# Routed tiles turned by VectorE from four strips, listed in the order of their rows, with the final loads released group by group

## The reference

```python
topk_p, topk_i = jax.lax.top_k(softmax(flat @ router_w.T), 2)      # 2 of 8 experts for each of 4096 tokens
topk_w = topk_p / topk_p.sum(-1, keepdims=True)
combine = zeros((T, 8)).at[arange(T)[:, None], topk_i].add(topk_w)
for e in range(8):                                                 # w_fc[e]: 512 x 128, w_proj[e]: 128 x 512
    out = out + (square(relu(flat @ w_fc[e].T)) @ w_proj[e].T) * combine[:, e:e + 1]
out = out + square(relu(flat @ shared_fc.T)) @ shared_proj.T
result = layernorm(flat + out)
```

## Time and profile before

| What | Value |
|---|---|
| Time, median of 3 runs | 490.98 us (490.75 to 491.0) |
| Profiled execution, first to last instruction (span) | 498.7 us |
| PE, DVE, ACT, POOL busy in the span | 454, 357, 354, 315 us |
| Mean DMA rate | 97 GB/s |
| 332.5 to 423.9 us (mostly full tiles): PE, ACT, DVE busy | 91.4, 61.9, 33.8 us |
| 470.4 us to the end (finish): length, PE busy | 28.3, 18.1 us |

### The profile page before, as it was taken

The page is one execution under the profiler, slowest core; times in us unless marked ns, Lnnn a source line. Parts: engine busy times, 40 slices in busy tenths (PEclk is TensorE's granted clock), DMA queues, the critical chain, the costliest instruction groups (busy, mean ns, idle before and its releaser), DMA issues.

```text
span 498.7 us, 7644 instructions
## 1 busy us (share of the span) xinstructions
PE 453.9 (91%) x2184; PEld 293.6 (59%) x2184; DVE 356.7 (72%) x873; ACT 354.5 (71%) x557; POOL 315.1 (63%) x285
## 2 busy tenths in 40 slices
PE   8997999999999988798898898489999999999983
PEld 5332444444344333455576675389999999899721
DVE  5898999999999999998688964353333333455246
ACT  3989999999999999815455555327667667566537
POOL 4754789999999999845566666604555455555421
PEclk9998999999999999989799999979999999999997
DMA  8031246654343434001111111131222222222095
GB/s 274 8 122 43 86 146 213 216 196 151 130 153 131 151 133 148 3 1 33 39 45 43 45 43 47 46 94 51 72 65 81 71 60 58 60 57 67 11 324 182
DMA packets 41193, 48.56 MB, mean 97 GB/s; under 512 B 5616, under 2 KB 25266, under 8 KB 41152
## 3 DMA queue, kind: packets, MB, share of 16 engines
q1 hardware_dynamic: 35792, 39.07, 23.8%
q0 software_dynamic: 5216, 8.70, 5.6%
q10 hardware_dynamic: 144, 0.31, 0.2%
HBM read 19.17 MB, written 29.11 MB: 97 GB/s over the span
## 4 chain that ended last, share of the span: by engine, by line
PE 40%; POOL 22%; DVE 16%; issue 8%; ACT 7%; DMA 2%; another core or an unknown queue 2%; DVEq 0%; POOLq 0%; SPq 0%; ACTq 0%
POOL memory_feat L495 17%; PE routed_ph L1500 13%; PE routed_po L1513 12%; PE dispatch_sph L998 4%; PE dispatch_spo L1008 3%; POOL memory_feat L503 2%; DVE memory_prod L769 2%; DVE memory_y_raw L778 2%; POOL memory_prod L518 2%; PE memory_nsum L620 1%; ACT finish_xo L1714 1%; PE routed_px L1488 1%; PE dispatch_plr L969 1%; DVE memory_feat L769 1%
## 5 line engine op out<-in xcount | busy, mean ns | idle before, releaser
L495 POOL TENSOR_TENSOR memory_feat<-memory_feat,memory_p_tok 128x1024 f32<-128x1024 f32 x64 | 125.9, 2063 | 17.1 <-ACT memory_feat L390 14.2
L620 PE MATMUL memory_nsum<-memory_feat,tri 128*128 128x512 f32 x256 | 118.1, 604 | 6.3 <-ACT memory_last_rows L403 2.4
L1476 POOL DMA_INDIRECT pick_scratch<-routed_ob,routed_xg x71 | 71.6, 1008 | 75.1 <-DVE routed_ob L1597 56.7
L1192 POOL DMA_INDIRECT table_scratch<-dispatch_xrow,dispatch_slot x64 | 61.9, 967 | 40.9 <-PE dispatch_sph L998 18.9
L620 PEld LDWEIGHTS memory_nsum<-memory_feat,tri 128*128 128x128 f32 x256 | 47.8, 192 | 65.1 <-issue 56.2
L1546 ACT ACTIVATE routed_rel<-routed_ph 128x512 f32<-128x512 f32 x71 | 42.3, 597 | 47.7 <-PE routed_ph L1500 46.7
L1513 PE MATMUL routed_po<-routed_w2c,routed_hid 128*128 128x128 f32 x568 | 71.3, 276 | 1.2 <-DVE routed_ob L1597 0.7
L1500 PE MATMUL routed_ph<-routed_xs,routed_w1c 128*128 128x256 f32 (+1 forms) x368 | 71.1, 337 | 1.2 <-DVE routed_w2c L1583 0.9
L1597 DVE TENSOR_SCALAR routed_ob<-routed_po,routed_xg 128x128 f32<-128x128 f32 x71 | 22.6, 347 | 69.2 <-issue 49.6
L769 DVE TENSOR_TENSOR memory_prod<-memory_nsum,memory_query 128x1024 f32<-128x1024 f32 x58 | 68.8, 1216 | 1.9 <-PE memory_nsum L620 1.8
L1513 PEld LDWEIGHTS routed_po<-routed_w2c,routed_hid 128*128 128x128 f32 x568 | 67.0, 192 | 1.9 <-issue 1.1
(11 more groups left out here) (192 smaller groups left out, 694.6 us busy)
## 6 DMA issues: line engine op xcount, KB each, us to landing
table_scratch<-memory_blank SPq DMA_DIRECT2D x68, 260.0 KB, 2.6
finish_pick<-pick_scratch SPq DMA_DIRECT2D x16, 256.0 KB, 6.0
routed_xg<-table_scratch SPq DMA_DIRECT2D x25, 130.0 KB
w<-w_up SPq DMA_DIRECT2D x9, 256.0 KB, 2.7
w<-w_down SPq DMA_DIRECT2D x9, 256.0 KB, 3.1
x_tok<-x SPq DMA_DIRECT2D x4, 512.0 KB, 3.7
out<-finish_xo SPq DMA_DIRECT2D x7, 256.0 KB, 2.3
routed_xg<-table_scratch SPq DMA_DIRECT2D x21, 65.0 KB
```

Of the source, the lines that this page charges most:

```text
L495: nc.gpsimd.tensor_tensor(v, v, pv, ALU.mult).then_inc(wfeat_done, 1)
L620: last = nc.tensor.matmul(nsum[:, o:o + 512], tri[:], feat[:, i % U, h, q * 512:(q + 1) * 512], start=True, stop=True)
L1192: nc.gpsimd.indirect_dma_start(out=table, in_=xrow[:, r, n, :], in_offset=None, out_offset=bass.IndirectOffsetOnAxis(ap=slot[:, r, n:n + 1 ...
L1476: nc.gpsimd.indirect_dma_start(out=pick_dram, in_=ob[:, u, h, :], in_offset=None, out_offset=bass.IndirectOffsetOnAxis(ap=xg[:, t % XU, h, ...
```

## The change

- **Loading.** A tile's 128 columns are loaded as four strips of 32 columns into `xb`. In a strip, the 32 rows of a block lie on 32 partitions and the blocks lie side by side, so that DVE's transpose, which turns each 32x32 block in place, gives the turned tile in one instruction (`xb` to `xs`). SP issues two strips two tiles ahead, ACT the other two: tiles 0 to 2 at the start and then tile `t + 3` at the end of its body for tile `t`, after `squared(t + 1)`. Each side reads the start row itself. The destination and weight columns go into `mark` by a third transfer on SP.
- **Turning.** PE's transposes, the PSUM tile `px` and ACT's copy are gone. DVE turns tile `t + 2` in its body for tile `t`, between the weight copies and the eviction.
- **Order of tiles.** The tables list all experts' first row blocks, then all second ones, so that early tokens' rows come in early tiles. Small products on PE (`totals`, `order`, `tiles`, `bases`, `turn_reach`) stand between the shared expert's last pieces, with short steps on DVE between them. For each group, `settle` holds the tile count at which its rows have been scattered.
- **Finish.** SP loads a group's picks when `kept` has reached the group's `settle` count, instead of after the last four scatters; POOL adds one to `kept` as each of the last four lands. Three shared sums are moved ahead of the routed stage on PE (`early_tensor`); the others are placed between the picks.

The diff, cut to this:

```diff
 @block.tensor
             rest()
+            fin.early_tensor(pe)
             rou.tensor(pe)
             fin.tensor(pe)
...
 # routed, SP
+            def strips(t):
...
+                if not early(t, XU):
+                    sp.wait_ge(turned, t - XU + 1)
+                n = height(t)
+                rows = table[bass.ds(first, n * P), :]
+                for j in range(BY_ACT):
+                    sp.dma_start(xb[j * SQ:(j + 1) * SQ, t % XU, 0:n * P].rearrange("a (i b) -> a i b", b=SQ),
+                                 rows[:, j * SQ:(j + 1) * SQ].rearrange("(i a) b -> a i b", a=SQ)).then_inc(loaded[t % XU], 16)
+
+            def marks(t, u):
+                first = sp.value_load(start[0:1, t:t + 1], min_val=0, max_val=TABLE - ROWS)
+                if not early(t, XU):
                     sp.wait_ge(scattered[u], passes(t - XU))
                 n = height(t)
-                sp.dma_start(xg[:, t % XU, 0:n], table[bass.ds(first, n * P), :].rearrange("(h p) c -> p h c", p=P)
-                             ).then_inc(loaded[t % XU], 16)
+                rows = table[bass.ds(first, n * P), :]
+                sp.dma_start(mark[:, t % XU, 0:n], rows[:, D:].rearrange("(h p) c -> p h c", p=P)).then_inc(marked[t % XU], 16)
+            def front():
+                strips(0)
+                strips(1)
+            def body(t, u):
+                if not beyond(t, 2):
+                    strips(t + 2)
+                marks(t, u)
...
 # routed, PE
             def up(t, u):
-                pe.wait_ge(x_kept, t + 1)
+                pe.wait_ge(turned, t + 1)
...
-                if not beyond(t, 2):
-                    turn(t + 2, (u + 2) % U)
                 down(t, u)
 # routed, ACT
+            def load(t):
...
+                first = act.value_load(start[0:1, t:t + 1], min_val=0, max_val=TABLE - ROWS)
+                if not early(t, XU):
+                    act.wait_ge(turned, t - XU + 1)
+                n = height(t)
+                rows = table[bass.ds(first, n * P), :]
+                for j in range(BY_ACT, STRIPS):
+                    act.dma_start(xb[j * SQ:(j + 1) * SQ, t % XU, 0:n * P].rearrange("a (i b) -> a i b", b=SQ),
+                                  rows[:, j * SQ:(j + 1) * SQ].rearrange("(i a) b -> a i b", a=SQ)).then_inc(loaded[t % XU], 16)
             def front():
-                keep_x(0, 0)
-                keep_x(1, 1)
+                act.wait_ge(dis.tabled, 1)
+                for r in range(2):
+                    act.wait_ge(dis.sent[r], 16 * NT)
+                for t in range(AHEAD):
+                    load(t)
...
             def body(t, u):
                 if not beyond(t, 1):
                     rectified(t + 1, (u + 1) % U)
-                if not beyond(t, 2):
-                    keep_x(t + 2, (u + 2) % U)
                 if not beyond(t, 1):
                     squared(t + 1, (u + 1) % U)
+                if not beyond(t, AHEAD):
+                    load(t + AHEAD)
 # routed, DVE
+            def turn(t):
+                dve.wait_ge(loaded[t % XU], 16 * STRIPS * (t // XU + 1))
+                if not early(t, 2):
+                    dve.wait_ge(up_done, parts(t - 1))
+                n = height(t) * P
+                nc.vector.transpose(xs[:, t % 2, 0:n], xb[:, t % XU, 0:n]).then_inc(turned, 1)
...
                     weights(t + 3, (u + 3) % U)
+                if not beyond(t, 2):
+                    turn(t + 2)
                 dve.wait_ge(down_done, t + 1)
+                dve.wait_ge(marked[t % XU], 16 * (t // XU + 1))
...
 # finish
-            for scattered, count in rou.scattered:
-                sp.wait_ge(scattered, count)
+            sp.wait_ge(dis.settled, 1)
             def load(g):
+                tiles = sp.value_load(settle[g:g + 1, 0:1], min_val=U + 1, max_val=TILES + U)
+                sp.wait_ge(rou.kept, tiles)
...
+        def early_tensor(pe):
+            pe.wait_ge(dis.added, NG - 1)
+            shared(0)
+            pe.wait_ge(dis.settled, 1)
+            shared(1)
+            shared(2)
...
                 picks(n)
+                if n == 0:
+                    pe.wait_ge(rou.rel_done, rou.banks)
+                if n + 3 == NG - 1:
+                    pe.wait_ge(rou.kept, TILES)
+                if n + 3 < NG:
+                    shared(n + 3)
...
+            for n, (scattered, count) in enumerate(rou.scattered):
+                pool.wait_ge(scattered, count)
+                nc.gpsimd.memset(tick[:, n:n + 1], 0.0).then_inc(rou.kept, 1)
```

More of the change, by code:

```diff
@@ L91, in build @@
         dis = dispatch(nc, c, early, mem, x_tok, y_all, ident, tri, rows, w_out, routerT, w_up, w_down, w1, w2,
-                       expert, start, table)
+                       expert, start, settle, table)
+        late = Late(nc, c, early.xrow, x_tok)
         rou = routed(nc, c, dis, ident, w1, w2, expert, start, table, pick_dram)
-        fin = finish(nc, c, rou, ident, y_all, eps, warm, pick_dram, out)
+        fin = finish(nc, c, late, dis, rou, ident, y_all, eps, warm, settle, pick_dram, out)
         block = c.enter_context(nc.Block())
@@ L920, in dispatch @@
         token = rows[:, P:P + NT]
+        pair = rows[:, P + NT:]
+        own, full_end, full_at = pair[:, 0:E], pair[:, E:E + 1], pair[:, E + 1:E + 2]
+        pair_e, full_row, half_at, half_row = [pair[:, E + n:E + n + 1] for n in range(2, 6)]
+        alike = pair[:, E + 6:]
         def group(g):
@@ L1071, in rest @@
                     down(g - 1, 3)
+                up(NG - 1, 0)
+                totals()
+                up(NG - 1, 1)
+                down(NG - 2, 0)
+                order(0)
+                down(NG - 2, 1)
+                tiles(0)
+                up(NG - 1, 2)
+                bases()
+                down(NG - 2, 2)
+                order(1)
+                up(NG - 1, 3)
+                tiles(1)
+                down(NG - 2, 3)
+                turn_reach()
                 for t in range(GT):
@@ L1482, in tensor @@
         def tensor(pe):
-            def turn(t, u):
-                pe.wait_ge(loaded[t % XU], 16 * (t // XU) + 16)
-                if not early(t, 1):
-                    pe.wait_ge(x_kept, t)
-                for h in range(height(t)):
-                    last = nc.tensor.transpose(px[:, h * P:(h + 1) * P], xg[:, t % XU, h, 0:D], ident[:])
-                last.then_inc(turned, 1)
             def up(t, u):
                 s = u % 2
-                pe.wait_ge(x_kept, t + 1)
+                pe.wait_ge(turned, t + 1)
                 pe.wait_ge(w_ready, t + 1)
@@ L1531, in scalar @@
         def scalar(act):
-            def keep_x(t, u):
-                act.wait_ge(turned, t + 1)
-                if not early(t, 2):
-                    act.wait_ge(up_done, parts(t - 1))
-                n = height(t) * P
-                nc.scalar.copy(xs[:, u % 2, 0:n], px[:, 0:n]).then_inc(x_kept, 1)
             def rectified(t, u):
@@ L1588, in front @@
                     weights(t, t)
+                for t in range(2):
+                    turn(t)
             def body(t, u):
```

281 lines of the change are left out of this document (156 added, 125 removed).

## The result

The changed kernel took 500.01 us (median of 4 runs, 499.6 to 501.76) beside 490.99 us for the kernel before on the same chip: ratio 1.0193, 95% interval 1.017 to 1.0217. The forecast was 488.0 us, with 477 to 499; both its sign and its range missed.

What follows compares the result with a forecast made beforehand. PE was taken to bound full tiles, a loop through ACT the half tiles, and late pick loads the finish. The terms -5.3 + 8.1 - 6.8 + 1.0 = -3.0 from 490.98 gave 488.0 us, range 477 to 499.

Steps and rivals of the forecast that it cites:

- The half tiles' term: Half tiles: a loop through ACT's strip loads sets 2.53 us a tile, 50.6 us in place of 42.5: +8.1 us.
- the sentence on strips: Tile loads: small pieces take 2.3 us a full tile, 1.2 a half tile, below the period, so cost nothing.
- The loop's own length: Half tiles: one round from Relu through ACT's issues, landing, turning and product takes 5.07 us for two tiles.
- The base: Half tiles before the change: 42.5 us from first to last Relu, taken from the profiled execution.
- Full tiles, -5.3: Full tiles: without PE's transposes a tile falls from 3.74 to 3.52 us, saving 5.3 us.
- Finish, -6.8: After the last tile: picks loaded early bring the first root 6.8 us earlier, and the shift carries through.
- Start, +1.0: Before the first routed product: ACT's issues and DVE's transpose behind weight copies cost between +0.5 and +3.2, taken as +1.0 us.
- SP's 2.7 us a tile: SP's queue: two register reads and three transfers take 2.7 us a tile; its lead from full tiles should hold.
- Rival 1: ACT's load waits for the activation ahead: 2.8 us a half tile, +8.1 in all, 499.1 us; chance 0.27.
- Rival 2: ACT's loop is shorter than its parts: half tiles at 1.9 us, -14.1 in all, 476.9 us; chance 0.19.
- Rival 3: Small pieces bind the DMA engines at 54 ns each: full tiles 4.6 us, +23.8 in all, 514.8 us; chance 0.04.

Runs made afterwards that it cites:

- e1: Changed kernel with ACT issuing its strips six tiles ahead in place of three: 484.55 us, 0.985 of the kernel before.
- e2: Changed kernel with ACT issuing its strips four tiles ahead in place of three: 485.14 us, 0.9885 of the kernel before.
- e7: Changed kernel with ACT issuing its strips two tiles ahead in place of three: 638.63 us, one run.
- e3: Changed kernel with no load of picks issued before the last tile is scattered: 502.72 us, 1.0206 of the kernel before.
- e4: Changed kernel with strips kept in full tiles, half tiles loaded whole by SP and turned by PE: 480.1 us, 0.9758 of the kernel before.
- e5: The kernel before, unchanged, profiled once more: 491.64 us, one run.
- e6: Changed kernel with all tiles loaded whole by SP and turned by PE, one early shared sum fewer: 486.4 us, 0.989 of the kernel before.
- e9: Changed kernel with all four strips of a tile issued by SP and none by ACT: 502.64 us, 1.0209 of the kernel before.

## Why the prediction was wrong

**The half tiles' term failed, +20.3 us in place of +8.1.** The mechanism named there, the loop through ACT's late strips, was the right one (e1, e2, e7 and the changed kernel show it at two, three, four and six tiles ahead). Its size was off, in three parts that add up to the 12.2 missing:

1. *The last five intervals, 7.4 us* (20.02 less 5 x 2.53), of which e3 shows 5.7 to be the collision with the loads of picks. The step that failed is the sentence on strips that costs the DMA engines' work at nothing because "no other transfer but the scatters runs there". The change itself puts the loads of picks there: the same prediction has them issued before the last eviction, counts that as a gain in the finish, and never asks what they do to strips that are needed as soon as they land. e3 takes the loads away and gets back 5.7; e4 keeps them and takes the late strips away, and nothing is lost. That strips queue behind the large transfers in the DMA engines fits the share of 0.88 and the unchanged 13 ns a packet; the rows don't show where they wait. The other 1.6 (14.28 less 12.65) is there without the loads of picks too, in e3.
2. *The loop's own length, 3.2 us* (41.15 less 15 x 2.53). A clean round takes 5.26 us in place of 5.07: from ACT's first issue to the turn 2.36, estimated 2.01, less small gains elsewhere; that is 1.7 us over 15 tiles. The other 1.5 is the one late strip, whose cause stays open.
3. *The base, 1.65 us.* The 42.5 us of before held stalls; 40.85 is what the kernel takes.

**Full tiles, -5.3: right.** The changed kernel's tile is 3.51 us, forecast 3.52. The table's -6.8 contains 2.3 us that are no gain of the change: the first 16 matmuls (two tiles) took 5.99 us in e5, where the granted clock was 0.50 from 323.6 to 327.6, and 3.72 in the changed kernel, where it was 1.00 from 324.0 to 328.0. The kernel before has 3.69 in the earlier trace rows, and e4, which starts like the changed kernel, 5.41. e4 against e6 gives 5.1. DVE's transpose took 445 ns for 256 columns and 312 for 128 by the groups of the changed kernel, where 0.4 and 0.25 us were estimated. The Trainium skill (VectorE: DVE Perf Modes, The three transpose paths) lists 311 ns for 128x128 in bf16, and f32 took as long here.

**Finish, -6.8: nearly right, -5.8.** The first root stands 6.6 us nearer to the last eviction (3.06 us behind it, 9.62 in e5); 0.8 is given back behind it, where root to end takes 19.2 us in place of 18.4.

**Start, +1.0: +0.4.** SP's 2.7 us a tile was right (in the changed kernel its pairs of strips start 2.72 us apart, at 440.33, 443.05 and 445.77 in the timeline), and so was that its lead holds, which is what let the loads of picks begin at 453.79.

**The rivals.** Rival 1 gave 499.1, 0.9 below the time that came, by a mechanism that did not come: ACT's first issue starts 1.34 us after the Relu, 0.08 after the Square's end, where a register load of 0.76 begun only then would have put it 0.76 behind. The issue itself does not wait for the Square either: in full tiles it starts before the second Square ends (410.48, the Squares run from 409.64 for 1.14 us). That the time agrees is chance. Its warning did count: the forecast had a gain only below 2.68 us a half tile, 0.15 above its own value, and the mean became 3.06. Rival 2 is out, but its 1.9 us is what e9 shows for as long as strips come early. Rival 3 is out: full tiles run at PE's pace with the DMA engines 0.42 busy, and ACT's strips took 14 ns a packet there, half of the 27 that the sum allowed for and a quarter of rival 3's 54. By the rule of the Trainium skill (DMA: Bandwidth & Descriptors, Specifications) pieces under 512 bytes miss line rate, and the share did rise, from 0.22 in e5's full tiles to 0.42, but not to where it binds.

The version to keep from these runs is e4: 0.9758 of the time before, with strips where the tile is long enough to hide the issues and whole loads where it is not.

## What to carry to other kernels

A load issued by an engine that also computes is part of the loop of that engine's work. Count how many tiles share one round, and issue one tile further ahead before anything else is tuned: here one tile turned 500 us into 485. When a change moves large transfers earlier, list what is in flight in their new place and how soon each of these is needed; the whole loads of e4, issued up to eight tiles ahead, were out before the loads of picks began and lost nothing, while strips issued two tiles ahead lost several us. Take the base of a difference by stage from an execution whose time is the median's.

## What was not expected of the hardware

Transfers issued one behind the other by one engine cost more than the issue itself: two strips took ACT 0.81 us (in the round from 425.32 above), four took SP 1.81. That is a step of 0.50 from one to the next, where the issue of one took 0.32 and the prediction counted 0.41. Now and then such a pair takes far longer, 1.83 us on ACT in e1 at 437.54; no row says why.

PE's granted clock followed its waiting. In e7, where PE is busy for 43.05 of 80 us, it is 0.70, between the two levels of 1.2 and 2.4 GHz, and a half tile's first product takes 1.96 us in place of 1.16. In the changed kernel, after PE had waited 3.35 us for the strip that was turned at 468.03, it is 0.59 from 469.0 to 473.0. A wait can thus cost twice. It need not: from 411.8 to 453.8 PE was busy for 32.29 of 42.00 us, and the clock stayed at 1.00.
